# Replanning the static order of all five engines in a two-layer adaptive-norm transformer kernel

## Time and profile before

| | us |
|---|---|
| median of 3 runs | 711.38 |
| lowest to highest | 710.27 to 713.83 |
| span of the profiled execution | 708.6 |
| PE busy, of which dummy matmuls | 619.4, 41.9 |
| DVE, ACT, POOL busy | 511.1, 385.6, 334.4 |

### The profile page before, as it was taken

How to read it: one execution, slowest core, us unless ns; L and a number is a source line. 1 busy time by engine, 2 the same in 40 slices (tenths; PEclk the granted TensorE clock), 3 DMA queues, 4 the chain that set the end, 5 groups by cost and what they waited for, 6 DMA issues and landing times. The chain is left out here.

```text
span 708.6 us, 12005 instructions
## 1 busy us (share of the span) xinstructions
PE 619.4 (87%) x3832; PEld 395.1 (56%) x3832; DVE 511.1 (72%) x1298; ACT 385.6 (54%) x861; POOL 334.4 (47%) x363
## 2 busy tenths in 40 slices
PE   8996887998899979979998799968798899789974
PEld 4665556997899779958654633212233344344332
DVE  5576959447458966155887389999888665958997
ACT  2342134678967557635699377737274456366410
POOL 5112287065478577767034153754214137106934
PEclk9998999999999989999999899979898899999998
DMA  8200325588678869999944615450501616421221
GB/s 339 91 1 1 107 103 179 174 280 286 212 258 274 284 216 332 296 295 302 291 151 104 163 45 105 119 107 28 89 1 45 134 52 128 125 91 53 53 59 30
DMA packets 47421, 106.40 MB, mean 150 GB/s; under 512 B 7440, under 2 KB 22608, under 8 KB 45824
## 3 DMA queue, kind: packets, MB, share of 16 engines
q1 hardware_dynamic: 41808, 94.82, 44.9%
q0 software_dynamic: 5120, 10.50, 5.1%
q10 hardware_dynamic: 432, 0.34, 0.2%
HBM read 80.26 MB, written 25.17 MB: 149 GB/s over the span
## 5 line engine op out<-in xcount | busy, mean ns | idle before, releaser
L1359 DVE TENSOR_REDUCE mxs<-PS 128x2 f32<-128x1024 f32 x128 | 152.2, 1221 | 60.0 <-PE PS L1687 59.5
L1027 ACT ACTIVATE bufa<-PS 128x512 f32<-128x512 f32 x256 | 134.8, 608 | 63.5 <-PE PS L1713 32.1
L986 ACT ACTIVATE bufb<-PS,bufb 128x128 f32<-128x128 f32 x368 | 103.6, 376 | 69.5 <-PE PS L1652 68.4
L1652 PE MATMUL PS<-bufb 128*128 128x128 f32 x736 | 101.2, 285 | 12.6 <-DMA bufb<-in_experts_dram 10.2
L1652 PEld LDWEIGHTS PS<-bufb 128*128 128x128 f32 x736 | 93.3, 199 | 20.7 <-issue 16.3
L1660 PE MATMUL PS<-bufb 128*128 128x128 f32 x736 | 101.2, 284 | 3.0 <-ACT bufb L986 3.0
L1660 PEld LDWEIGHTS PS<-bufb 128*128 128x128 f32 x736 | 93.8, 199 | 7.2 <-ACT bufb L986 4.1
L842 POOL DMA_INDIRECT slots_in<-bufb x64 | 65.1, 1017 | 63.8 <-DVE bufb L1305 45.4
L1703 PE MATMUL PS<-stk 108*128 108x512 bf16 x256 | 87.0, 400 | 6.5 <-ACT bufa L1027 3.6
L1687 PE MATMUL PS<-stk 96*128 96x512 bf16 x256 | 80.9, 408 | 8.2 <-DVE mxs L1359 6.2
L853 POOL DMA_INDIRECT bufb<-slots_out,bufb x64 | 62.1, 971 | 50.9 <-issue 43.8
(11 more groups left out here) (302 smaller groups left out, 1031.6 us busy)
## 6 DMA issues: line engine op xcount, KB each, us to landing
bufb<-in_experts_dram SPq DMA_DIRECT2D x92, 514.0 KB, 5.2
slots_out<-bufb SPq DMA_DIRECT2D x30, 256.0 KB, 4.5
stk<-split SPq DMA_DIRECT2D x56, 128.0 KB, 7.6
bufb<-slots_in SPq DMA_DIRECT2D x25, 256.0 KB, 3.3
split<-terms SPq DMA_DIRECT2D x8, 768.0 KB, 3.8
slots_in<-hb SPq DMA_DIRECT2D x2, 1536.0 KB, 9.0
stk<-split SPq DMA_DIRECT2D x8, 384.0 KB, 4.6
X<-in_x_dram SPq DMA_DIRECT2D x4, 512.0 KB, 6.5
```

The costliest lines, as they stand in the source:

```text
L986: last = nc.scalar.activation(hs[:, n % HR, fc, :], ps[:, P * fc:P * fc + P], ACT.Gelu_apprx_tanh, bias=ws[:, n % WR, F + fc:F + fc + 1])
L1027: nc.scalar.activation(probs[:, i % PR, j, :], psum("s2", i, j), ACT.Exp, scale=DH1 ** -0.5)\
L1359: nc.vector.tensor_reduce(mxs[:, gr % 2, 2 * j:2 * j + 2, h], psum("s1", i, j).rearrange("p (c n) -> p c n", c=2), axis=AX.X, op=ALU.max)\
L1652: last = nc.tensor.matmul(ps[:, P * fc:P * fc + P], ws[:, n % WR, P * fc:P * fc + P], xq[:, q % 2, P * x:P * x + P], start=True, stop=True)
```

## The change

Nothing in `build()` changes. The planner's numbers and its rules do:

1. `LENGTH`, one number per step, becomes two: `BUSY` (how long the step holds its engine) and `SEEN` (from its start until another engine can use its result). For example `PE s1` was 0.45 and is busy 0.43, seen 0.60; `ACT bh` was 1.14 and is busy 1.02, seen 1.14; `SP bw` was 2.1 and is 1.05.
2. `LATENCY` and the lags in the plan give way to `LANDS`, the time from the issue to the landing of each kind of transfer, and `SERVED`, how long each keeps one common transfer queue: a transfer lands no earlier than the ones issued before it allow.
3. `HOP`, 0.1 us for every crossing, is now set by the engine that waits (0.03 to 0.13); on PE a step may follow its own engine's producer 0.2 us before its end.
4. An exp after a gelu, or the reverse, costs `TABLE_LOAD`, 1.3 us on ACT.
5. After more than 3.0 us (`COOL`) idle, PE's steps take twice as long for 4.0 us (`WARM`).
6. A step takes a PSUM bank only when everything that the step that frees the bank waits for, other than what follows from the taking step itself, is done (`before_take`).
7. `NEAR` goes from 0 to 0.2 us.
8. `URGENCY`, 20 numbers by kind, becomes `PRIORITY`, by engine, kind and pair, some 400 numbers between -1971 and 1975.

```diff
-LENGTH = {
-    ('PE', 'pc'): 1.84, ('DVE', 'pc'): 0.44, ('PE', 'pm'): 2.0, ('ACT', 'pm'): 1.01, ('PE', 'pr'): 1.0,
...
+BUSY = {
+    ('ACT', 'akv'): 1.57, ('ACT', 'aot'): 0.96, ('ACT', 'aq'): 2.06, ('ACT', 'atr'): 1.81, ('ACT', 'bgt'): 0.26, ('ACT', 'bh'): 1.02,
...
+SEEN = {
+    ('ACT', 'aot'): 1.07, ('ACT', 'atr'): 1.93, ('ACT', 'bh'): 1.14, ('ACT', 'btr'): 1.45, ('ACT', 'by'): 0.5, ('ACT', 'cpq'): 1.27,
...
-LATENCY = {
-    ('SP', 'bxl', 'PE', 'bxt'): 4.5, ('SP', 'cst', 'PE', 's1'): 8.5,
+LANDS = {
+    ('POOL', 'bga'): 2.8, ('POOL', 'bsc'): 2.9, ('POOL', 'rga'): 3.4, ('POOL', 'rsc'): 4.8, ('SP', 'bw'): 2.95,
+    ('SP', 'bxl'): 2.5, ('SP', 'byo'): 1.75, ('SP', 'ckp'): 4.0, ('SP', 'cst'): 7.3, ('SP', 'cto'): 3.35,
...
-HOP = 0.1
-URGENCY = {
-    'akx': -10, 'an2': 160, 'anm': 10, 'aq': 10, 'bn2': 80, 'btr': -10, 'byo': 80, 'ckp': 40, 'cn4': -80, 'cpt': 20,
...
-NEAR = 0
+SERVED = {
+    'bga': 1.0, 'bsc': 1.0, 'bw': 1.6, 'bxl': 0.85, 'byo': 0.85, 'ckp': 1.0, 'cst': 3.4, 'cto': 2.3,
...
+PRIORITY = {
+    ('ACT', 'akv'): (-249, 276, 239, -26), ('ACT', 'aot'): (-192, -327, 696, -116), ('ACT', 'aq'): (83, -503, 1685, -510), ('ACT', 'atr'): (1361, 558, -254, 830),
...
+    ('POOL', 'rga'): (276,), ('POOL', 'rsc'): (-961,), ('SP', 'bw'): (1475, -779, -530, -616), ('SP', 'bxl'): (-598, 956, 289, 142),
...
+TABLE = {"blg": 1, "ex": 1, "aq": 1, "akv": 1, "bh": 2}
+TABLE_LOAD, COOL, WARM = 1.3, 3.0, 4.0
+NEAR = 0.2
...
+            if lag > 1.0 or d[0] == "SP" and d[:2] in LANDS:
+                lag = LANDS.get(d[:2], lag) + HOP[eng]
+            elif d[0] == eng:
+                lag = -0.2 if eng == "PE" else 0.0 if eng in ("POOL", "SP") else 0.03
+            else:
+                lag = HOP[eng]
...
-        rank[k] += URGENCY.get(k[1], 0.0)
+        rank[k] += PRIORITY[k[:2]][part(k)]
+    before_take = {k: [d for d, _ in ops[giver[k]][2] if d[:2] != k[:2] and all(x != k for x, _ in ops[d][2])]
+                   for k in ops if ops[k][3]}
...
+                if ops[k][3]:
+                    if any(d not in done for d in before_take[k]):
+                        continue
+                    t = max(t, min(vacant[ops[k][3]]))
+                if e == "ACT" and TABLE.get(k[1], table) != table:
+                    t += TABLE_LOAD
...
+        if e == "PE":
+            if idle[k] > COOL:
+                slow = t + WARM
+            if t < slow:
+                busy, seen = 2 * busy, seen + busy
+        elif e == "ACT":
+            table = TABLE.get(k[1], table)
+        clock[e], end = t + busy, t + seen
+        if SERVED.get(k[1]) and e in ("SP", "POOL"):
+            end = max(queue, end)
+            queue = end + SERVED[k[1]]
```

More of the change, by code:

```diff
@@ L62, in same_rows @@
     return n - 3 if n == 4 * (PAIRS - 1) + 1 else n - 4
-LENGTH = {
-    ('PE', 'pc'): 1.84, ('DVE', 'pc'): 0.44, ('PE', 'pm'): 2.0, ('ACT', 'pm'): 1.01, ('PE', 'pr'): 1.0,
[L67 to L87, removed]
-}
@@ L100, in plan, with part @@
+TABLE = {"blg": 1, "ex": 1, "aq": 1, "akv": 1, "bh": 2}
+TABLE_LOAD, COOL, WARM = 1.3, 3.0, 4.0
+NEAR = 0.2
+PER_PAIR = {"s1": 16, "mx": 16, "msp": 4, "mt": 4, "mtc": 4, "s2": 16, "ex": 16, "pv": 4, "pvo": 4, "cpq": 2, "cpt": 2, "cpv": 2,
+            "cto": 2, "cst": 2}
+def part(k):
+    return k[2] // PER_PAIR.get(k[1], 1)
 def plan():
@@ L105, in op @@
         key = eng, kind, i, j
-        length = LENGTH.get((eng, kind), length)
-        deps = [a if len(a) == 2 else (a, 0.0) for a in after if a]
-        deps = [(d, LATENCY.get((d[0], d[1], eng, kind), lag + (HOP if d[0] != eng else 0.0))) for d, lag in deps]
+        busy = BUSY.get((eng, kind), length)
+        deps = []
+        for d, lag in ((a, 0.0) if len(a) == 4 else a for a in after if a):
+            if lag > 1.0 or d[0] == "SP" and d[:2] in LANDS:
[4 more added lines that the diff above has]
+                lag = HOP[eng]
+            deps.append((d, lag))
         if (eng, kind) in last:
-            deps.append((last[eng, kind], 0.0))
+            deps.append((last[eng, kind], -5.0))
         last[eng, kind] = key
-        ops[key] = (length, deps, take, give)
+        ops[key] = (busy, SEEN.get((eng, kind), busy), deps, take, give)
         return key
@@ L329, in arrange @@
 def arrange(ops, start):
-    users, left, est, rank = {k: [] for k in ops}, {}, {}, {}
-    for k, (_, deps, _, _) in ops.items():
+    users, left, est, rank, giver = {k: [] for k in ops}, {}, {}, {}, {}
+    for k, (_, _, deps, _, give) in ops.items():
         left[k], est[k] = len(deps), 0.0
@@ L370, in arrange @@
         t, _, k = first
-        length, _, take, give = ops[k]
+        busy, seen, _, take, give = ops[k]
+        e = k[0]
         if take:
@@ L375, in arrange @@
             vacant[take][n], count[take][n] = 1e9, count[take][n] + 1
-        idle[k] = t - clock[k[0]]
-        clock[k[0]] = t + length
+        idle[k] = t - clock[e]
+        if e == "PE":
[9 more added lines that the diff above has]
+            queue = end + SERVED[k[1]]
         if give:
             cls, n, _ = use[give]
-            vacant[cls][n] = t + length
-        order[k[0]].append(k[1:])
-        ready[k[0]].remove(k)
+            vacant[cls][n] = end + HOP["PE"]
+        order[e].append(k[1:])
+        ready[e].remove(k)
+        done.add(k)
         for u, lag in users[k]:
-            est[u], left[u] = max(est[u], t + length + lag), left[u] - 1
+            est[u], left[u] = max(est[u], end + lag), left[u] - 1
             if not left[u]:
```

65 lines of the change are left out of this document (58 added, 7 removed), and 22 rows, old and new, of tables (BUSY, PRIORITY, SEEN).

## The result

The kernel after takes 720.61 us (median of 4 runs, 717.25 to 723.25), the kernel before 712.61 us in the same comparison: a ratio of 1.0115, interval 1.0073 to 1.0156. It is slower by about 8 us. I had forecast 686 us and a range that ended at 716. The profiled execution took 718.92 us, its span is 716.9 us.

What follows compares the result with a forecast made beforehand. PE was taken as near its work (87% busy) but not at it, the bound varying by stage. Gains 6 + 17 + 4 + 3 - 4.6 = 25.4 us took the span from 708.6 to 683.2; plus 2.8, 686 us, range 660 to 716.

Steps and rivals of the forecast that it cites:

- long waits and the clock: PE behind the opening: a third of 53.2 us of gaps and lost clock goes, 17 us; bounds 0 and 35.
- Opening, -6: Before the first expert matmul: other pairs' work and dummies leave pair 0's way, 6 us less; bounds 0 and 11.
- The clock's price: PE after long waits: 28.7 us of lost clock hang mostly on seven waits, some 4.1 us each.
- a wait of 3.5 us costs about 7.6 us: PE behind the opening: a long wait costs its own length plus some 4.1 us of lost clock.
- Table loads, -4: ACT from 360 to 392 us: half of six table loads go, 4 us less; bounds 0 and 7.7.
- End, -3: Last 24.6 us: DVE selections of the first half done before, 3 us less; bounds 0 and 5.2.
- My sign for it: End of the kernel: less than 24 us between the last L1713 and the end would show the gain.
- DVE and POOL, +4.6: On the path: two more meetings of DVE and POOL steps, unseen by the plan, 4.6 us more; bounds 0 and 18.
- Weights late: Rival, chance 0.11: weight loads queued behind other transfers on SP come late, two more such waits, 718 us.
- DVE and POOL meeting more often: Rival, chance 0.04: eight more meetings on the path at 2.28 us, no long wait removed, 717 us.
- A chance of 0.15 for slower: Whole kernel: the two slower rivals together, 0.11 for late weights and 0.04 for DVE and POOL.
- a plan that sees what COOL, SERVED and before_take describe should avoid most of what it sees: PE behind the opening: reason given for taking 17 us of the 53.2 us of gaps and lost clock.

Runs made afterwards that it cites:

- the clock held: Dummy matmuls ahead of 12 TensorE steps that waited over 1.5 us, in the kernel before (ratio 1.0005) and the kernel after (2 us, overlapping intervals).

## Why the prediction was wrong

The step that failed first is the term for long waits and the clock, -17 us, by far the largest of the sum. In its place stand -2.0 us. It was wrong in both halves: the waits were exchanged for others, and no run shows that their clock has the price I gave it.

- *Opening, -6.* It is +8.4 us in length (up to 11.0 in the other traces) and about +4.6 net. The priorities do what I allowed for in the lower bound, spare other pairs instead, and more: 179 dummies of 44.1 us against 165 of 41.9, other pairs' `apr` and `an2` ahead of the ranks. The plan itself puts the first expert matmul at 123.1 us against 121.2 for the old order. It never meant to shorten the opening, and the bound of 0 was on the wrong side of it.
- *Long waits and clock, -17.* The stretch is 2.0 us shorter. Long waits ahead of the last `pv` are 17.9 us against 24.5, but PE's idle time is 64.7 against 62.5: the planner split and moved it. The clock's price, 4.1 us a wait, was 28.7 us divided by seven waits; the rows don't pair them so neatly. The 1.13 us of L1652, my example of the full clock, stand right behind a wait of 4.06 us; the clock was 0.60 only from 318 to 322 us. In the kernel after, L1702 took 1.06 us behind a wait of 4.08, with 0.74 in the 2 us from 258 and 0.50 in the next 2. And a slowdown is no cost where a wait follows: with the clock held, the two clean stretches are as long as before. There "a wait of 3.5 us costs about 7.6 us" should have been 3.5 at most; how much it is where DVE leads, which does 225 of 288 us in the third stage, stays open.
- *Table loads, -4.* Four loads fewer, 5.1 us of ACT, and nothing of it seen in the time: the stretch where ACT led is no longer full.
- *End, -3.* It is 1.9 us longer, with the longest wait of all (5.43 us, at 695.92) in it. My sign for it, under 24 us from the last `pv`, was misread besides: that stretch was 32.5 us before.
- *DVE and POOL, +4.6.* Right in size. By the difference between each DVE instruction's time and the usual time of its kind where POOL worked beside it, I count 36.0 us of stretching before and 42.0 after, and DVE's busy time is up by 9.8. Whether these 6 us divide the orders is not settled. Cutting GpSimd's instructions short left the two further apart (1.0170), shrinking its work made them level (0.9958).
- *The rivals.* Weights late named 718 us, the nearest, but PE waited for them 8.6 us in all against 10.2, so that is luck. DVE and POOL meeting more often named 717 us and had a chance of 0.04. More stretching there is, but it is 6.0 us over the whole kernel, not 18.2 on the path, and which part of it costs time is the open question above. Neither names the longer opening. A chance of 0.15 for slower was far too low for a change whose only evidence of gain was that a plan could now see more.

Behind the terms stands one assumption, "a plan that sees what COOL, SERVED and before_take describe should avoid most of what it sees". It did avoid it, on its own clock: 680.9 to 650.3 us. The chip gave none of it. Putting the measured lengths of steps into the planner's model, on the same two orders, hints at where the promise thins out. With DVE's it is 22.4 us (714.1 to 691.7), with DVE's and POOL's 15.0 (714.3 to 699.3), with every engine's 0.3 (715.2 to 714.9). This is arithmetic on a model, which no run tests, and it hangs on how a step's length is read from a trace: if only the deviation from the usual length of its kind is put in, some 26, 24 and 15 us are left. Either way part of the promise goes with steps of DVE and POOL, and more with PE's, whose lengths at the lower clock the clean stretches show to be partly a consequence of waits.

Still open: why orders of the new planner stand 60 to 72 us above its clock and those with the old rest 32 to 37. Shrinking GpSimd takes 3 us off the distance of the orders with dummies in both (1.0073 to 1.0028) and 11 without (1.0115 to 0.9958), so it is the one suspect left for the 8 us; whether by its length or by holding VectorE is not shown. What was not tried: the planner with GpSimd and VectorE as one resource where they meet.

## What to carry to other kernels

A planner's gain on its own clock is a promise about its model: before believing it, put the measured lengths of both orders into the model and see what is left (here 30.6 us shrank to 15 or to 0.3, by how lengths are read), and time a neighbour or two, since a clock can rank its own orders fairly and still be 30 us off between families. Price a slow TensorE clock by filling the waits and timing it, not by the granted clock, and see in the trace that the filling ends before the wait does: here half of it did not. Cut long GpSimd element-wise instructions to the size of VectorE's where the two overlap: here that took 6.7 us off the old order with no other change, and 1.7, within the noise, off the new one.
